# Finding the row maxima of the first 512 attention queries inside the layer before

## The reference

```
f = xf @ Wf + bf                       # keys,    32 channels
g = xf @ Wg + bg                       # queries, 32 channels
hh = xf @ Wh + bh
attn = softmax(einsum('bnd,bmd->bnm', g, f), axis=-1)
o = einsum('bnm,bmc->bnc', attn, hh) @ Wo + bo
out = gamma * o + xf
```

## Time and profile before

| | us |
|---|---|
| three runs | 4747.96, 4747.84, 4744.28 |
| median | 4747.84 |
| the profiled execution, own time | 4750.32 |
| its span, first to last instruction | 4747.8 |
| PE busy | 4274.5 (90%) |
| DVE busy | 3988.9 (84%) |
| POOL busy | 3660.8 (77%) |
| ACT busy | 3334.4 (70%) |
| mean granted TensorE clock | 0.959 |

### The profile page before, as it was taken

One profiled execution on the slowest core, in us unless ns is written; L12 is line 12 of the kernel. 1 busy time (PEld: TensorE's weight loads), 2 busy tenths in 40 slices (PEclk: granted clock), 3 DMA queues, 4 the chain that ended last, 5 costly groups with the idle time before them and its releaser, 6 DMA issues. The chain is left out here.

```text
span 4747.8 us, 77692 instructions
## 1 busy us (share of the span) xinstructions
PE 4274.5 (90%) x23360; PEld 3006.3 (63%) x23360; DVE 3988.9 (84%) x7545; ACT 3334.4 (70%) x5896; POOL 3660.8 (77%) x3476
## 2 busy tenths in 40 slices
PE   3788888888888888888988699999999999999998
PEld 2455555555555555555554478887888788878887
DVE  2999999999999999999999477777777677777775
ACT  3888888888888888888887255555555555555555
POOL 1998989898888989898988167766666666666666
PEclk7899999999999999999999799999999999999999
DMA  2011111110111110101110400031001300040000
GB/s 75 12 49 33 49 33 49 33 49 33 49 33 49 33 49 33 49 33 49 37 44 26 143 13 22 19 87 54 21 17 31 107 20 21 22 119 17 17 21 18
DMA packets 139261, 198.03 MB, mean 42 GB/s; under 512 B 18346, under 2 KB 106388, under 8 KB 138644
## 3 DMA queue, kind: packets, MB, share of 16 engines
q1 hardware_dynamic: 138900, 193.76, 12.9%
HBM read 114.02 MB, written 79.69 MB: 41 GB/s over the span
## 5 line engine op out<-in xcount | busy, mean ns | idle before, releaser
L1270 POOL TENSOR_TENSOR pl<-probs,ph 128x512 fp32r<-128x512 f32 x1024 | 1322.6, 1292 | 645.6 <-PE ps_o L1380 323.2
L731 POOL TENSOR_TENSOR dec<-dt,rates 128x384 f32<-128x384 f32 x1536 | 1494.7, 1001 | 163.1 <-ACT dt L626 99.2
L1473 ACT ACTIVATE ph<-ps_s 128x512 fp32r<-128x512 f32 x1024 | 612.7, 598 | 906.6 <-PE ps_s L1363 906.6
L1485 DVE TENSOR_REDUCE part_max<-ps_m 128x1 f32<-128x512 f32 x1024 | 687.5, 688 | 391.9 <-PE ps_m L1346 391.9
L1372 PE MATMUL ps_o<-ph,vh 128*128 128x512 f32 x2048 | 812.2, 397 | 15.0 <-ACT o_ch L1459 9.6
L1372 PE MATMUL ps_o<-ph,vl 128*128 128x512 f32 x2048 | 805.2, 393 | 0.0
L1514 DVE TENSOR_TENSOR ps_a<-probs,ps_a 128x512 f32<-128x512 f32 x992 | 681.4, 687 | 40.6 <-ACT probs L1475 35.1
L744 POOL TENSOR_TENSOR y_tok<-y_tok,dec 128x384 f32<-128x384 f32 x512 | 512.7, 1001 | 185.8 <-DVE dec L892 150.9
L1380 PE MATMUL ps_o<-pl,vh 128*128 128x512 f32 x2048 | 635.3, 391 | 0.0
L1475 ACT ACTIVATE probs<-ps_s 128x512 f32<-128x512 f32 x1024 | 607.2, 593 | 0.0
L902 DVE SCALAR_TENSOR_TENSOR psS<-u,bc,psS 128x384 f32<-128x384 f32 x1024 | 594.6, 611 | 1.1
(11 more groups left out here) (164 smaller groups left out, 7280.1 us busy)
## 6 DMA issues: line engine op xcount, KB each, us to landing
values_d<-hid SPq DMA_DIRECT2D x64, 512.0 KB, 4.3
xf<-in_x_dram SPq DMA_DIRECT2D x128, 128.0 KB
xb<-in_x_dram SPq DMA_DIRECT2D x128, 128.0 KB
residual_d<-xb SPq DMA_DIRECT2D x32, 512.0 KB, 2.7
vh<-values_d SPq DMA_DIRECT2D x32, 512.0 KB, 7.2
vl<-values_d SPq DMA_DIRECT2D x32, 512.0 KB, 8.5
res<-residual_d SPq DMA_DIRECT2D x32, 512.0 KB, 3.3
out_dram<-res SPq DMA_DIRECT2D x128, 128.0 KB
```

The costliest lines, as they stand in the source:

```text
L731: last = nc.gpsimd.tensor_tensor(dec[:, q % RING, j - 1, :], dt[:, par, d, token_of(d, j), :], rates[:, d, n, :], ALU.mult)
L1270: nc.gpsimd.tensor_tensor(pl[:, m % DEPTH, :], probs[:, m % DEPTH, :], ph[:, m % DEPTH, :].bitcast(F32), ALU.subtract).then_inc(pl_ok, 1)
L1473: nc.scalar.activation(ph[:, m % DEPTH, :], ps_s[m % 2][:, :], ACT.Exp).then_inc(ph_ok, 1)
L1485: nc.vector.tensor_reduce(part_max[:, qt, kc:kc + 1], ps_m[r % 2][:, :], AX.X, ALU.max).then_inc(max_out, 1)
```

## The change

The 32 products and reductions for the maxima of chunk 0 are done in the last body of layer 0, in the three `psF` banks. SP loads the first image's keys and the first queries from memory into `rates` and `x_win`, whose last readers it waits for. PE issues the products and DVE the reductions after steps named in two tables. The tiles are plain fp32, not fp32r. `part_max` lives on into layer 1, where the loop of 32 products and reductions is dropped and the semaphores are raised by hand; the order of layer 1's first loads changes: queries 0, keys and values of part 0, queries 1, `f_max`, then parts 1 to 7 and the residual.

```diff
+EARLY_PE = {"": 3, "out1": 3, "w10": 3, "w11": 3, "w12": 3, "w13": 3, "w20": 4, "w21": 4, "x1t1": 2, "fg0": 2, "v1": 2}
+EARLY_DVE = {"": 3, "ln2_mean": 3, "ln2_shift": 12, "w20": 4, "w21": 6, "fg0": 2, "v1": 2}
...
+        early_keys = rates[0:SPLIT, :, :, :].rearrange("p d n c -> p (d n c)")[:, 0:PER_IMAGE * TOK].rearrange(
+            "p (j n) -> p j n", j=PER_IMAGE)
+        early_queries = x_win[0:SPLIT, :, :].rearrange("p t c -> p (t c)")[:, 0:TOK]
+        part_max = keep["part_max"]
...
+            def load_early():
+
+                sp.wait_ge(fg_stored, 96 * (TILES - 1))
+                sp.wait_ge(arg_ok, CHAINS * TILES)
+                sp.wait_ge(u_mul, 2 * T * TILES)
+                sp.dma_start(early_keys, f_d[0:PER_IMAGE].rearrange("j r n -> r j n")).then_inc(early_loaded, 16)
+                sp.dma_start(early_queries, g_d[0]).then_inc(early_loaded, 16)
+
             def body(k, par, part):
                 g = k - 1
+                if part == "back":
+                    load_early()
...
+            def early_max(n):
+
+                for _ in range(n):
+                    r = next(early)
+                    if r == 0:
+                        pe.wait_ge(early_loaded, 32)
+                        pe.wait_ge(front_out, len(NEXT_JOBS) + (TILES - 1) * len(FRONT_JOBS) + len(OWN_JOBS))
+                        pe.wait_ge(r_ok, CB * TILES)
+                    if r >= FRONT_BANKS:
+                        pe.wait_ge(early_out, r - FRONT_BANKS + 1)
+                    qt, kc = r // PER_IMAGE, r % PER_IMAGE
+                    pe.matmul(psF[r % FRONT_BANKS][:, :], early_queries[:, qt * P:(qt + 1) * P],
+                              early_keys[:, kc, :], start=True, stop=True).then_inc(early_full, 1)
+
             def body(k, par, part):
+                if part == "back":
+                    early_max(EARLY_PE[""])
                 for step, tile, at in steps(PE_ORDER, k, part):
                     if is_back(step):
                         back(step, tile, 1 - par)
+                        if part == "back":
+                            early_max(EARLY_PE.get(step, 0))
...
+            def early_reduce(n):
+
+                for _ in range(n):
+                    r = next(early)
+                    qt, kc = r // PER_IMAGE, r % PER_IMAGE
+                    dve.wait_ge(early_full, r + 1)
+                    nc.vector.tensor_reduce(part_max[:, qt, kc:kc + 1], psF[r % FRONT_BANKS][:, :], AX.X,
+                                            ALU.max).then_inc(early_out, 1)
+
             def body(k, par, part):
+                if part == "back":
+                    early_reduce(EARLY_DVE[""])
...
                         back(step, tile, 1 - par)
+                        if part == "back":
+                            early_reduce(EARLY_DVE.get(step, 0))
...
+            load_queries(0, 0)
+            load_keys_values(0, 0)
+            load_queries(1, 1)
             load_keys_max(0)
-            load_queries(0, 0)
-            load_queries(1, 1)
-            for j in range(PER_IMAGE):
+            for j in range(1, PER_IMAGE):
                 load_keys_values(0, j)
             load_res(0, 0)
...
-                            scores_max(c + 1, 1 - par, half + par, r, img + 1 if at == "turn" else None)
+                            scores_max(c + 1, 1 - par, half + par, r, img + 1 if at == "turn" else 0 if at == "first" else None)
...
-            for r in range(KEYS):
-                scores_max(0, 0, 0, r, 0)
+            pe.sem_inc(max_full, KEYS)
+            pe.wait_ge(g_loaded[0], 16)
             spread_max(0)
...
-            dve.sem_inc(max_out, 2)
+            dve.sem_inc(max_out, 2 + KEYS)
...
             dve.wait_ge(const_ok, 4)
-            for r in range(KEYS):
-                reduce_max(0, r)
             for what in range(4):
                 finish_max(0, what, 0)
```

More of the change, by code:

```diff
@@ L339, in layer0 @@
         res_stored = sem("res_stored")
+        early_loaded = sem("early_loaded")
+        early_full = sem("early_full")
+        early_out = sem("early_out")
         apart = sem("apart")
@@ L563, in back @@
                 mm.then_inc(back_full, 1)
+            early = iter(range(PER_IMAGE * T))
+            def early_max(n):
[10 more added lines that the diff above has]
+                              early_keys[:, kc, :], start=True, stop=True).then_inc(early_full, 1)
             def body(k, par, part):
+                if part == "back":
+                    early_max(EARLY_PE[""])
                 for step, tile, at in steps(PE_ORDER, k, part):
@@ L1186, in layer1 @@
         pl = sb("pl", [P, DEPTH, TOK], F32R)
-        part_max = sb("part_max", [P, QT, PER_IMAGE])
+        part_max = keep["part_max"]
         row_max = sb("row_max", [P, QT])
@@ L1592, in build @@
             "gamma": ctx.enter_context(nc.sbuf_tensor("gamma_sb", [P, 1], F32)),
+            "part_max": ctx.enter_context(nc.sbuf_tensor("part_max", [P, T, PER_IMAGE], F32)),
             "res_bc": ctx.enter_context(nc.sbuf_tensor("res_bc", [P, C], F32)),
```

## The result

The changed kernel takes 4779.19 us (median of 6 runs, 4773.08 to 4781.05), the kernel before 4746.11 (6 runs, 4744.17 to 4749.63): a ratio of 1.0066, with a 95% interval of 1.0054 to 1.0077. It is 33.1 us slower; 33.2 was forecast. The profiled execution of the changed kernel has a span of 4775.0 us, 27.2 more than before, although its layer 0 up to the last tile's back steps was 3.6 shorter. The single executions of a kernel scatter by 5 to 8 us here, and those of the kernel before by 11 in the 27 runs beside the first experiments, so differences under about 3 us are read from the stages of the traces and not from the medians. A trace is one execution too, and where the same stage differs from trace to trace, that is said.

The account below looks back on a forecast made before the run. Bounds: layer 0's dependent back steps, layer 1's start with DMA saturated, then PE, 98% busy. Layer 0 ends 41.1 us later, layer 1 gains 7.9: 33.2 slower, 4781.0 us; own range 4768 to 4789, widened to 4758 to 4792.

Parts of the forecast that it names:

- stall before the first product: Layer 0's last body: PE waits for the early load of keys and queries, landing 2637.0, ahead of yt0; 16.8 us.
- out to h2t (three products, reductions): Three products after out1 in layer 0's last body: PE's idle hides 2.6 us, DVE's reductions add 1.6.
- twelve in w1: Twelve products after w10 to w13 in layer 0's last body: 10.3 us less 0.87 of PE idle, 9.4.
- tail of layer 0, sum: Stall and exposed products in the last tile's back steps together make layer 0 end 41.1 us later.
- gain in layer 1 up to the restart: Layer 1, chunk 0: first score 29.1 us earlier, but POOL's wait for the residual stops PE; 9.8 us gained.
- lost to the clock at the restart: Layer 1, chunk 0: PE starts again at the low clock for 3.7 us and loses 1.9; net gain 7.9.
- rival B: Layer 0: four-engine backlog doesn't hold the early load; stall 13.0, or 3.7 less with warmer clock; 4774 to 4777.
- One product 0.86 us: PE in layer 0: a plain fp32 product of 512 columns takes two records, 0.86 us at full clock, 1.72 at 1.2 GHz.
- Rival A: Layer 1, chunk 0: the residual lands before 2698.2, so its wait doesn't bind; +13 us, 4761; chance 0.10.
- Rival C: Both load queues: early load lands at 2625.4, residual before 2698.2; not slower, 4748; chance 0.05.
- Rival D: Layer 1, chunk 0: PE's restart meets further waits; the gain falls to 3 us, 4786 to 4789; chance 0.10.

Follow-up runs that it names:

- the first experiments: The earliest edits of the changed kernel, to the order of its loads; the kernel before took 4747.3 us beside them.
- experiments 1 to 4: Changed kernel with, in turn: residual load behind f_max, 4759.0 us; early load one body sooner, 4757.6; both, 4737.8; early load ahead of the xb loads, 4773.4.
- Experiment 2: Changed kernel with the early load of keys and queries issued one body sooner, behind the residual's store: 4757.6 us.
- experiment 4: Changed kernel with the early load issued ahead of the last tile's xb loads and values stores: 4773.4 us.
- Experiments 5 and 6: Changed kernel without the 32 products and reductions, the early load and its wait kept: 4756.5 us; changed kernel with the products in fp32r: 4767.0 us.
- experiment 1: Changed kernel with the residual load of chunk 0 issued right behind f_max instead of behind all eight parts: 4759.0 us.
- experiments 8 and 9: Changed kernel with early load sooner, fp32r products, memset wait moved behind the broadcast, residual load behind part 1: 4729.64 us; then also POOL's long memsets cut into eight: 4736.3.
- experiment 7: Changed kernel with early load one body sooner, residual load behind f_max and products in fp32r: 4728.65 us, ratio 0.9964 to the kernel before.

## Why the prediction was right

The steps, with the measured size from the two traces:

| term | forecast, us | measured, us |
|---|---|---|
| stall before the first product | 16.8 | 16.0 |
| first three products | 4.7 | 5.3 |
| yt steps | 0 | 0.4 |
| out to h2t (three products, reductions) | 1.6 | 0.7 |
| twelve in w1 | 9.4 | 8.3 |
| eight at w20 and w21 | 6.0 | 5.8 |
| two after x1t1 | 0.9 | 0.8 |
| two after fg0 | 1.7 | 1.9 |
| v0 to the end of the block | 0 | -0.8 |
| tail of layer 0, sum | 41.1 | 38.5 |
| gain in layer 1 up to the restart | 9.8 | 9.4 |
| lost to the clock at the restart | 1.9 | 1.8 |

Each is a difference of starts: the stall, say, is 2632.62 less 2616.61, which is yt0's old start of 2620.20 moved by the 3.6 us of drift. The tail came out 2.6 us shorter than forecast. 1.1 of it is the w1 stretch, where I had left the clock as before: seven of the 16 L535 records ran slowly before, four of the L556 records after. 0.9 is around the projection: 0.6 by its records (7.04 us for 7.62), the rest by DVE's reductions, which cost the chain 1.3 and not 1.6. 0.8 is the stall and 0.8 the store that ends the block, less 1.0 at the start of the tail. The clock's part is not firm: with the same products the w1 stretch took 19.0 to 19.8 us in experiments 1 to 4, and the projection up to 8.24. Layer 1's gain is from block start to the sixth low part: 56.5 before (2729.50 less 2673.01), 47.05 after (2754.93 less 2707.88). By the traces the sum is 38.5 - 7.7 = 30.8, and with the drift of -3.6 it is the 27.2 of the spans; the medians differ by 33.1. That the medians' difference was met to a tenth is luck within this scatter; the mechanism, two waits on loads and a chain that the products lengthen, is what the traces bear out.

Three readings in the prediction are off; none moves the forecast by more than 0.2 us. The low clock of the L535 run could give back 3.0 us at most (seven records of 0.86 instead of 0.43), not the 3.7 that rival B uses. The residual's landing at 2717.5 with 0.75 and 1.29 behind it is 2719.5, not 2719.7. And what waits behind the residual is POOL's sixth low part, that of block 5, not the fifth.

*The stall.* The load's place in SP's queue, its size and the backlog were each needed for the 16.8. Experiment 2 took the whole stall away; experiment 4 took 3.1 us of it with what stood ahead of the load and 3.8 with the place; the size was not varied. By the nearest single row (10.1 us) the stall would have been 13.0.

*One product 0.86 us.* From the first of L599's six records to the next step it is 2.6 us for three products. Experiments 5 and 6 show the share: the products cost the tail 21.4 us, 15.5 of it by plain fp32.

*Rival A* (the residual's wait doesn't bind) was wrong, and experiment 1 is what it would have been: 4759.0, forecast 4761. *Rival B* (the backlog doesn't hold the load, stall 13.0) was wrong by the stall of 16.0, though its time lay inside the forecast's range. *Rival C* (DMA has much more to give) fell with the 12.6 us landing. *Rival D* (further waits at the restart) did not come: POOL's four low parts after the residual ran back to back in 4.97 us and PE lost only the clock.

Not settled: why layer 0 up to the tail was 3.6 to 6.5 us shorter in five of the eleven traces than in the other six, with nearly the same instructions there, and what decides which clock the output projection gets.

## What to carry to other kernels

Work moved from an exposed stage into another must be priced by that stage's own gaps: here 32 products had 27 us of length and met about 6 us of gaps on a dependent chain, though PE stood idle a third of the time. Ask of each load which wait it ends after the change and what stands ahead of it in its queue: a new load and one that the removed work had hidden stopped PE for 34.7 us (16.0 and 18.7), and reordering the two gave back 41.4 us of the median, with the low clock that had followed each wait. Before cutting a start shorter, look up what lands last there: in experiments 8 and 9 PE waited 3.1 and 5.1 us for a load that had not held it in experiment 7.

## What the runs showed of the hardware that was not expected

DVE's four 128x128 `tensor_scalar` operations from SBUF to SBUF took 6.75 us beside two POOL memsets of 3.5, 1.11 beside short ones (16 in 7.8 us), and 0.87 alone. The Trainium skill (SBUF — State Buffer, "SBUF: two separate sides") says that the port pair shared by DVE and GpSimd is locked for a whole instruction by whichever starts first, a GpSimd operation or a DVE one in a two-port mode, and that the other fully waits. The trace agrees: of the four operations three lasted 2.82 to 3.61 us, each up to the end of a memset. Which mode DVE ran in, it doesn't show. Before and after the change DVE's wait for the memsets had kept the two apart.

Behind the last tile's `xb` loads and the values stores DMA ran on at a share of 0.26 and 0.30. The early load's last 192 KB, queued behind these transfers and its own 1.5 MB of keys, landed after 12.6 us, and after 9.5 with the keys alone ahead of them.
